# The 2048 x 2048 adjacency matrix enters on-chip memory through GpSimd's casting DMAs instead of float32 staging places

## What is computed

```python
x = layernorm(x + L0(x, adj))      # adj @ (x @ W) + b, eight heads side by side
x = layernorm(x + L1(x, adj))      # graph attention, 4 heads: softmax(leaky_relu(src+dst) + adj) @ (x @ W), mean
x = layernorm(x + L2(x, adj))      # two graph convolutions: relu([x, adj @ x] @ W + b), with a residual
x = layernorm(x + L3(x, adj))      # relu(D^-1/2 (adj + I) D^-1/2 @ x @ W)
```

## Time and profile before

| | |
|---|---|
| median of 3 runs | 685.37 us (685.23 to 685.78) |
| the profiled execution | 686.34 us, of which the profiled span is 684.6 us |
| TensorE matmul busy | 672.8 us, 98% of the span |
| VectorE, ScalarE, GpSimd busy | 76%, 57%, 24% |
| granted TensorE clock | 0.999 of full speed |
| SyncE's DMA queue | 39.37 MB |
| GpSimd's DMA queue | 7.34 MB |
| casts of the adjacency | 14 on ScalarE, 2 on VectorE |

### The profile page before, as it was taken

How to read it: one execution, slowest core, us unless ns; L and a number is a source line. 1 busy time by engine, 2 the same in 40 slices (tenths; PEclk the granted TensorE clock), 3 DMA queues, 4 the chain that set the end, 5 groups by cost and what they waited for, 6 DMA issues and landing times.

```text
span 684.6 us, 14405 instructions
## 1 busy us (share of the span) xinstructions
PE 672.8 (98%) x5326; PEld 511.9 (75%) x5326; DVE 522.6 (76%) x965; ACT 389.2 (57%) x499; POOL 163.9 (24%) x260
## 2 busy tenths in 40 slices
PE   8989999999999999999999999999999999999996
PEld 6878744788888888888888888884444468886444
DVE  5247668998998989989899898999454425874685
ACT  6556448798979889898898989643101000222000
POOL 4269627501001000010100001564021102442222
PEclk9999999999999999999999999999999999999999
DMA  8999431003003030030300303013021110211011
GB/s 334 380 404 302 83 105 33 16 1 77 18 33 61 26 66 0 31 61 31 61 0 31 61 0 63 1 36 72 17 54 24 24 23 18 40 39 32 32 51 42
DMA packets 48154, 47.65 MB, mean 70 GB/s; under 512 B 36017, under 2 KB 42225, under 8 KB 45937
## 3 DMA queue, kind: packets, MB, share of 16 engines
q1 hardware_dynamic: 45664, 39.37, 18.8%
q0 software_dynamic: 2016, 7.34, 5.7%
q10 hardware_dynamic: 432, 0.39, 0.2%
HBM read 29.23 MB, written 2.13 MB: 46 GB/s over the span
## 4 chain that ended last, share of the span: by engine, by line
PE 89%; DMA 4%; DVE 3%; ACT 2%; POOL 0%; issue 0%; ACTq 0%; SPq 0%; POOLq 0%
PE ps L725 16%; PE ps L727 16%; PE ps L726 16%; PE ps L571 16%; PE ps L561 9%; PE ps L573 6%; PE ps L574 6%; DMA arena<-in_adj 4%; PE ps L674 3%; DVE arena L1004 1%; ACT adj L413 1%; DVE ring_a L1048 1%; DMA arena<-in_x_turned 1%; DVE ring_hl L1053 0%; ACT ring_a L468 0%; ACT arena L447 0%
## 5 line engine op out<-in xcount | busy, mean ns | idle before, releaser
L727 PE MATMUL ps<-arena,ring_hl 128*128 (+1 forms) x1024 | 279.6, 273 | 0.0
L725 PE MATMUL ps<-arena,ring_hl 128*128 (+1 forms) x1024 | 278.8, 272 | 0.1
L726 PE MATMUL ps<-arena,ring_hl 128*128 (+1 forms) x1024 | 278.6, 272 | 0.0
L1048 DVE SCALAR_TENSOR_TENSOR ring_a<-rho,gam,ring_a 128x1024 f32<-128x1024 f32 x128 | 165.8, 1296 | 18.1 <-ACT ring_a L468 18.1
L1053 DVE TENSOR_TENSOR ring_hl<-ring_a,ring_hl 128x1024 f16<-128x1024 f32 x128 | 157.9, 1235 | 4.6 <-ACT ring_hl L482 4.6
L482 ACT ACTIVATE ring_hl<-ring_a 128x1024 f16<-128x1024 f32 x128 | 135.4, 1058 | 44.3 <-PE ps L727 27.4
L468 ACT ACTIVATE ring_a<-adj,shift 128x1024 f32<-128x1024 bf16 x128 | 146.0, 1141 | 0.0
L573 PE MATMUL ps<-arena,adj 128*128 128x257 f16 (+1 forms) x512 | 113.1, 273 | 3.0 <-ACT adj L413 3.0
L574 PE MATMUL ps<-arena,adj 128*128 128x256 f16 x512 | 113.1, 273 | 0.0
L571 PE MATMUL ps<-arena,adj 128*128 128x512 f16 x496 | 111.6, 379 | 0.0
L725 PEld LDWEIGHTS ps<-arena,ring_hl 128*128 128x128 f16 x1024 | 100.0, 98 | 13.0 <-DVE arena L1004 0.6
(11 more groups left out here) (109 smaller groups left out, 586.2 us busy)
## 6 DMA issues: line engine op xcount, KB each, us to landing
arena<-in_adj SPq DMA_DIRECT2D x16, 1024.0 KB, 10.7
x<-y POOLq DMA_DIRECT2D x14, 512.0 KB, 5.2
rho<-s_scratch SPq DMA_DIRECT2D x8, 512.0 KB, 3.7
x<-in_x SPq DMA_DIRECT2D x4, 512.0 KB, 17.0
out_x<-x SPq DMA_DIRECT2D x16, 128.0 KB, 1.7
arena<-in_x_turned SPq DMA_DIRECT2D x2, 512.0 KB, 6.2
arena<-in_L_gnn_W SPq DMA_DIRECT2D x1, 1024.0 KB, 11.3
arena<-in_L_gnn_a SPq DMA_DIRECT2D x1, 1024.0 KB, 13.3
```

Source lines behind the costliest of these rows:

```text
L725: nc.tensor.matmul(acc, hi, v_hi, start=(jt == 0), stop=False)
L726: nc.tensor.matmul(ps[:, b, 0:D], hi, v_lo, start=False, stop=False)
L727: ins = nc.tensor.matmul(acc, lo, v_hi, start=False, stop=(jt == T - 1))
L1048: nc.vector.scalar_tensor_tensor(a, rho[:, q, :], gam[:, at(h, 1), jt], a, op0=ALU.max, op1=ALU.mult)\
```

## The change

The staging places, the casts and their semaphores go. GpSimd issues 16 DMAs, one for each piece, that read float32 from the device's main memory and write bfloat16 straight into `adj`. `adj` now has the layout [partition, row tile, contraction tile, column], so that a piece is two runs of 1024 elements in each partition; the host orders the piece accordingly. Each piece has its own semaphore, and TensorE waits for that. SyncE holds back its loads of the bias and x until certain pieces have landed. GpSimd issues pieces 0 and 2 before its five low parts of `xt`, pieces 1, 3, 4, 5 between and behind them, then 6 and 7, 8 to 11 each behind an `add_b0`, and 12 to 15 ahead of its loop over tiles. ScalarE makes the high half of `w1` behind `gat_hi(4)`, ahead of that loop before. The row tiles of `rest` in the first layer are written out, with no loop.

```diff
-        adj = sb("adj", [P, T, N], BF16)
+        adj = sb("adj", [P, T, T, P], BF16)
...
-        STAGES = 4
-        SW = JH * LW
-        stage = part(arena, (PSET, PSET + STAGES * SW), F32, "p (s w) -> p s w", s=STAGES)
-        w1f = part(arena, (PSET + STAGES * SW, PSET + STAGES * SW + K2 * H * D), F32, "p (k h f) -> p k h f", k=K2, h=H)
-        o = PSET + STAGES * SW + K2 * H * D
+        o = PSET + T * D + K2 * H * D
+        w1f = part(arena, (PSET + T * D, o), F32, "p (k h f) -> p k h f", k=K2, h=H)
         w1ff = w1f.rearrange("p k h f -> p k (h f)")
-        xts = part(arena, (PSET + STAGES * SW, PSET + STAGES * SW + T * D), F32, "p (t c) -> p t c", t=T)
+        xts = part(arena, (PSET, PSET + T * D), F32, "p (t c) -> p t c", t=T)
...
-            for n in FIRST_LOADS:
-                load_adj(n)
+            sp.wait_ge(ld_adj[FIRST_LOADS[1]], 16)
             sp.dma_start(bias0, b0_in.rearrange("(a n) -> a n", a=1).partition_broadcast(P)).then_inc(ld_b, 16)
 
             def load_x(r):
                 sp.dma_start(x[:, r * R:(r + 1) * R, :], xr[:, r * R:(r + 1) * R, :]).then_inc(ld_x[r], 16)
             load_x(0)
-            load_adj(4)
-            load_adj(5)
+            sp.wait_ge(ld_adj[3], 16)
             load_x(1)
-            sp.wait_ge(s_lo, T)
+            sp.wait_ge(ld_adj[6], 16)
             sp.dma_start(w1f, w1_in.rearrange("(k p) (h f) -> p k h f", p=P, h=H)).then_inc(ld_w1, 16)
             sp.dma_start(abc.rearrange("p h s f -> p (h s f)"),
                          a_in.rearrange("h f a -> a (h f)").partition_broadcast(P)).then_inc(ld_a, 16)
-            load_adj(6)
-            load_adj(7)
             load_x(2)
-            load_adj(8)
+            sp.wait_ge(ld_adj[10], 16)
             load_x(3)
-            for n in range(9, NL - 2):
-                load_adj(n)
-            for n in range(NL - 2, NL):
-                load_adj(n)
...
-            for n in (1, 3, 4, 5):
-                cast_n(n)
-            w1_hi(0)
-            w1_hi(1)
-            cast_n(6)
-            CAST = cast_n
-            behind = {0: [(CAST, 7)], 2: [(CAST, 8)], 3: [(CAST, 9)], 4: [(CAST, 10)], 5: [(CAST, 11)], 6: [(CAST, 12)],
-                      7: [(CAST, 13)], 9: [(CAST, 14)], 10: [(CAST, 15)], 12: [(was_hi,)]}
+            behind = {4: [(w1_hi, 0), (w1_hi, 1)], 12: [(was_hi,)]}
...
-                nc.scalar.activation(ring_a[:, jt % SLOTS, :], adj[:, jt, q * CH:(q + 1) * CH], ACT.Exp,
+                nc.scalar.activation(ring_a[:, jt % SLOTS, :].rearrange("p (b c) -> p b c", b=BANKS), adj[:, q * BANKS:(q + 1) * BANKS, jt, :], ACT.Exp,
...
-                lhs = adj[:, j, at(it * P, P)]
+                lhs = adj[:, at(it, 1), j, :].rearrange("p a c -> p (a c)")
...
-                if knext in PLACES:
+                if knext in PLACES or a == 0:
...
-            def columns_cast(j):
+            def columns_loaded(j):
                 if j == 0:
                     pe.wait_ge(s_one, 1)
                 if j % JH == 0:
-                    pe.wait_ge(*cast_done(STAGES // 2 + j // JH))
-            joint(0, 0, lambda t: 0, columns_cast)
-
-            def cast_ready(t, u, half):
-
-                pe.wait_ge(s_cast_act, t + (half + 1 - u % 2 - STAGES // 2))
-            rest(0, None, cast_ready)
+                    for n in (j // JH, 2 + j // JH):
+                        pe.wait_ge(ld_adj[n], 16)
+            joint(0, 0, lambda t: 0, columns_loaded)
+
+            def piece_loaded(t, u, half):
+
+                pe.wait_ge(ld_adj[t // 2 * 2 + half], 16)
+            rest(0, None, piece_loaded)
...
-            casts_after = {8: 0, 11: 2}
             for t in range(T):
                 take(0, t, t % R)
-                if t in casts_after:
-                    cast_n(casts_after[t])
...
+            adj_n = adj_in.rearrange("c h p w -> (c h) p w")
+
+            def load_adj(n):
+                js = slice((n % 2) * JH, (n % 2 + 1) * JH)
+                nc.gpsimd.dma_start(adj[:, n // 2 * 2:n // 2 * 2 + 2, js, :],
+                                    adj_n[n].rearrange("p (i j c) -> p i j c", i=2, j=JH)).then_inc(ld_adj[n], 16)
+            pool.wait_ge(*xt_loaded(4))
+            load_adj(FIRST_LOADS[0])
+            load_adj(FIRST_LOADS[1])
             pool.wait_ge(s_lo, CHUNKS[5][0])
-            for lo, hi in CHUNKS[5:]:
+            later_loads = {0: FIRST_LOADS[2], 1: FIRST_LOADS[3], 3: 4, 4: 5}
+            for n, (lo, hi) in enumerate(CHUNKS[5:]):
                 pool.wait_ge(s_hi, hi)
                 nc.gpsimd.tensor_sub(xt[:, lo:hi, D:2 * D], xts[:, lo:hi, :], xt[:, lo:hi, 0:D]).then_inc(s_lo, hi - lo)
+                if n in later_loads:
+                    load_adj(later_loads[n])
+            load_adj(6)
+            load_adj(7)
             pool.wait_ge(ld_b, 16)
 
             def add_b0(t):
@@ -1169,6 +1135,8 @@
                 nc.gpsimd.tensor_tensor(x[:, t, :], x[:, t, :], bias0, ALU.add).then_inc(s_xb, 1)
             for t in range(2 * R):
                 add_b0(t)
+                if t >= R:
+                    load_adj(t + 4)
...
+            for n in range(12, NL):
+                load_adj(n)
```

More of the change, by code:

```diff
@@ L153, in graph_stack @@
         ld_xt = [sem(f"ld_xt{i}") for i in range(6)]
-        ld_adj = [sem(f"ld_adj{i}") for i in range(STAGES)]
+        ld_adj = [sem(f"ld_adj{i}") for i in range(NL)]
         ld_w0 = [sem(f"ld_w0{i}") for i in range(K2)]
@@ L219, in xt_loaded @@
             return ld_xt[next(n for n, (lo, hi) in enumerate(XT_LOADS) if lo <= t < hi)], 16
-        def cast_done(n):
-            if n < STAGES:
-                return (s_cast_act if n % 2 else s_cast), n // 2 + 1
-            return s_cast_act, n + 1 - STAGES // 2
-        def cast_of(n):
-            src = stage[:, n % STAGES, :].rearrange("p (j w) -> p j w", j=JH)
-            return adj[:, (n % 2) * JH:(n % 2 + 1) * JH, (n // 2) * LW:(n // 2 + 1) * LW], src
         PLACES = {3: {5: [0], 6: [1, 2], 7: [3, 4], 8: [5, 6], **{t: [t - 2] for t in range(9, T)}},
@@ L259, in _ @@
                     sp.dma_start(w0f[:, 1, :], w0r[:, 1, :]).then_inc(ld_w0[1], 16)
-            adj_n = adj_in.rearrange("c h p w -> (c h) p w")
-            def load_adj(n):
-                if n >= STAGES:
-                    sp.wait_ge(*cast_done(n - STAGES))
-                sp.dma_start(stage[:, n % STAGES, :], adj_n[n]).then_inc(ld_adj[n % STAGES], 16)
-            for n in FIRST_LOADS:
-                load_adj(n)
+            sp.wait_ge(ld_adj[FIRST_LOADS[1]], 16)
             sp.dma_start(bias0, b0_in.rearrange("(a n) -> a n", a=1).partition_broadcast(P)).then_inc(ld_b, 16)
@@ L611, in last_tile @@
                     for j in range(T):
-                        lhs = adj[:, j, (T - 1) * P:T * P]
+                        lhs = adj[:, T - 1, j, :]
                         for half, first in ((0, j == 0), (1, False)):
@@ L1271 @@
         host["adj"].T.reshape(halves, n // (halves * p), p, blocks, n // blocks).transpose(3, 0, 2, 1, 4)
-        .reshape(blocks, halves, p, -1))
+        .reshape(blocks, halves, p, n // (halves * p), -1, p).transpose(0, 1, 2, 4, 3, 5).reshape(blocks, halves, p, -1))
     host["L0_gnn_W"] = np.ascontiguousarray(host["L0_gnn_W"].transpose(1, 0, 2))
```

7 lines of the change are left out of this document (removed).

## The result

The changed kernel is slower: 698.69 us median of 4 runs (696.01 to 698.92) against 685.58 us for the kernel before on the same chip (685.23 to 686.57), ratio 1.018 [1.0157, 1.0203]. The prediction named 684.2 us, with a range of 682 to 702 us: the time is inside the range, but the sign is the other one, and the loss is 13.1 us where the likeliest case had a gain of 1.2 us.

What follows compares the result with a forecast made beforehand. TensorE was taken to bound the kernel; layer 1 would start at the later of its own 76.4 us and `was` at 77.5 us, against 78.7 us: -1.2 us, so 684.2 us from 685.37 us, range 682.0 to 702 us.

Steps and rivals of the forecast that it cites:

- the likeliest case: The forecast itself: issues of 0.95 to 1.2 us, casts at plain speed, 684.2 us (683.2 to 685.8), chance 0.36.
- 1.2 us were feared: Issues ahead of and among GpSimd's low parts: joint stage starts at 19.8 us, not 18.64 us, +0.6 to +3.9 us.
- about 27 us: Landing of x rows 4 to 7, asked for at about 22 us, before GpSimd's next adds ahead of its loop.
- part (b): Issues on GpSimd ahead of its loop over tiles: loop start moves from 34.92 us to 38.2 us.
- L: Start of GpSimd's loop over tiles, put at 38.2 us; `was` ready 39.3 us later, at 77.5 us.
- dear issues: Rival: GpSimd issues from 1.2 us up delay its loop; at 1.62 us, +5.3 us, 690.7 us; chance 0.20.
- The issue price: GpSimd's time for each of sixteen added issues: between 0.86 and 1.62 us, taken as 1.05 us.
- light issues: Rival: GpSimd issues cost 0.86 us each, loop starts at 36.7 us, -2.7 us, 682.7 us; chance 0.22.
- Casting transfers slow: Rival: from 3.5 us a piece TensorE waits; 4.5 us gives 699.7 us, 5.3 us gives 712.5 us; chance 0.22.
- VectorE's normalisation would lengthen an issue: By a two-port rule, the four issues of pieces 12 to 15 grow by up to 0.4 us each; sum about +0.4 us.
- The sum: TensorE starts layer 1 at 77.5 us against 78.7 us, moving the end one for one: -1.2 us, 684.2 us.
- the 3.0 us of waits for casts: TensorE's three waits for ScalarE's casts in the joint aggregation, expected to go: -3.0 us.

Runs made afterwards that it cites:

- Eight issues: Kernel before, with eight small DMAs into an unread tile issued by GpSimd where the changed kernel issues pieces 8 to 15: 687.86 us.
- the two with moved products: Products 0 and 1 ahead of the loop (all inputs early, x in 4 KB runs): 693.71 us; products two tiles forward (the version at piece 3): 691.37 us.
- the two with all inputs early: Changed kernel, SyncE asking for bias, x rows 0 to 7, `w1f`, `abc` straight behind the turned features: 693.88 us; with 4 KB runs of x too: 694.22 us.
- eps on ScalarE: The version at piece 3, with the addition of eps to the variance moved from GpSimd to ScalarE: 688.33 us.
- its layout: Kernel before with only the new layout of `adj`, staging places and casts kept: 685.63 us.
- late x: Kernel before, with SyncE asking for x rows 4 to 7 behind piece 7 instead of piece 5: 693.02 us.
- one queue: Changed kernel with bias, x, `w1f` and `abc` also issued by GpSimd, in the order of the kernel before, 23 issues instead of 16: 690.18 us.
- the issues first: Changed kernel, with GpSimd issuing pieces 8 to 15 behind piece 7, ahead of its wait for x: 696.11 us.
- x in 4 KB runs: Changed kernel, with x stored by the host so that four rows lie together, one 4 KB run per partition for each load: 695.82 us.
- `w1f` early: Changed kernel, with only `w1f` and `abc` asked for ahead of the wait for piece 2: 700.42 us.
- the version at piece 3: Changed kernel, with x rows 0 to 7 asked for at once and `w1f` and `abc` when piece 3 has landed instead of piece 6: 688.98 us.

## Why the prediction was wrong

**Right, by the rows.** TensorE's projections end where they did (18.6 us): moving pieces 0 to 5 among the low parts cost nothing, where 1.2 us were feared. The cast runs at the plain rate, 272 packets a piece at 638 in 6 us, 2.56 us for 2.6, and TensorE's L532 never waits for a piece. The layout is free. From the start of the loop to `was` it takes 85.36 - 46.10 = 39.3 us, the prediction's number to 0.1 us. And the end does hang on `was`, 0.1 us ahead of layer 1.

**Wrong: "about 27 us".** The step that failed is the term for the landing of x rows 4 to 7 in part (b), "which then share the DMA queues: about 27 us". It was 37.5 us, 10.5 us off. The request came as predicted; the transfers of x were sized as if each had its turn behind the bytes ahead of it, as in one queue at 0.41 MB/us, rows 0 to 3 (taken as landed by 22 us, used at 31.66 us) as well as rows 4 to 7. They stand in a second one, and there their packets of 1 KB go one for one with packets of 4 KB. With 37.54 us in place of 27 and an issue of 0.74 us, the prediction's own formula gives L = 37.54 + 4 x (0.70 + 0.74) + 4 x 0.74 = 46.3 us (46.10 measured) and `was` at 85.6 us. The mechanism had been named, at the end of the rival of dear issues ("a later landing of x rows 4 to 7 ... works at the same place, 1 us for 1 us"), but its size was never worked out, and it was given no chance of its own.

**The issue price erred the safe way.** 1.05 us were taken, 0.74 us came. So the price of the rival "light issues" (0.86 us) was the nearest and that of "dear issues" the wrong one; the loss came from the place that both shared. Eight issues by themselves cost 2.1 us in the kernel before. "Casting transfers slow" is excluded by 0.418 MB/us, and with it goes the reason for which the range reached beyond 691 us. Whether VectorE's normalisation would lengthen an issue no run shows: it stood behind the eight issues and not beside them.

**Missing: two steps behind `was`.** The sum took the end to move with the start of layer 1, one for one. It moved 6.9 us, and attention 12.96 us. First, the turned tiles: in the kernel before TensorE starts 2 us behind `was`, and never waits for one (an unbroken chain); where it starts right behind `was`, it meets tiles that come from the same loop a little later, 3.0 us in the changed kernel, 2.5 to 3.2 us in seven of its variants. The distance orders all the runs but the two with moved products: 0.1 us behind `was`, 2.5 to 3.2 us of waits; 1.0 to 1.1 us (the two with all inputs early), 1.6 us; 1.8 us (eps on ScalarE), 0.6 us; 1.9 to 2.0 us (the kernel before, its layout, late x and eight issues), 0 to 0.3 us. So no variant won the 3.0 us of waits for casts either: with `was` at 77.3 us and layer 1 at 77.40 us, attention began at 123.70 us, not before 122.20 us. Second, the clock: behind the waits of 2.55 and 0.46 us the 1.2 GHz level held from 96 to 102 us, +2.8 us. In the variant with waits of 1.97 and 0.50 us, the stretch behind them had the full clock:

```profile
88.00:92.00 4.00, 3.95 (x22) 1.88 (x23) 0.00 (x0) 0.60 (x1) 0.00 (x0) 1.00 0.17 33
```

and the remainder is gone: from the start of layer 1 to attention 46.30 us, against 43.65 us before plus 2.5 us of waits; in the changed kernel 49.70 us against 43.65 + 3.0. What decides whether the clock falls is open, and the length of the waits is not it: with 2.9 us of them (one queue) it stayed at 1.00, and of two variants with 2.5 us each, the issues first and x in 4 KB runs, one fell and the other did not (96 to 98 us in both):

```profile
96.00:98.00 2.00, 2.00 (x6) 0.76 (x5) 0.00 (x0) 0.60 (x1) 0.00 (x0) 0.50 0.01 1
...
96.00:98.00 2.00, 1.83 (x15) 0.92 (x16) 0.00 (x0) 0.01 (x1) 0.00 (x0) 1.00 0.34 66
```

Executions of one kernel differ too: of the changed kernel's four, three took 698.64 to 698.92 us at a mean clock of 0.989 to 0.992 and one 696.01 us at 0.994. These 2.7 us are the size of the clock's piece, though the short one has no trace.

**A regularity that holds it together.** In the kernel before the first product starts at 42.60 us and `was` is ready at 76.60 us:

```profile
42.60 1.27 POOL L1180 TENSOR_TENSOR ring_a<-arena 128x512 f32<-128x512 f32 x1
```

That is 34.0 us. After the change: 85.36 - 51.35 = 34.0 us. In ten runs in which only inputs or issues moved it lies between 34.0 and 34.1 us, from a first product at 45.51 us (the eight issues) to 54.85 us (`w1f` early); the version at piece 3 took 35.5 us, with 1.45 us of waiting for later rows of x. So the chain through GpSimd has no slack in that stretch: everything that delays its first product arrives at `was` in full.

**Shown and not shown.** Shown by single edits in the kernel before: late x alone loses 7.0 us, the issues alone 2.1 us, the layout nothing. Shown in the changed kernel: asking earlier for x and for `w1f` and `abc` together regains 9.7 us, x alone 3.9 us, `w1f` and `abc` alone, at the very front, nothing. That x is slow for its share of packets is shown by the equal counts and by the 4 KB runs (8.8 for 14.0 us). Argued from the traces, and not shown by an edit, is that the waits for turned tiles come from the start right behind `was`, and that the clock's 2.8 us belong to the stop. Open is what keeps the best variants 2.5 to 3.5 us behind in the median: their traces show attention only 1.1 and 1.5 us later, in executions of 687.39 and 687.60 us that were among the shortest. Some of it may be the eight issues, the turned tiles, the pieces or the clock; no run took the eight issues out of a version in which all inputs were in time.

## What to carry to other kernels

When a large stream moves to another engine's queue, work out anew when everything that stays in the old queue lands: what was ordered by position is now ordered by the waits that replace it, and where two queues are full, the one with the smaller packets falls behind (here a quarter of the engines' time for 1 KB against 4 KB). Look for the engine without slack (here GpSimd from its first product on), list its inputs in the order in which it needs them, and give each a landing time; if the first is mended the next one shows, as `abc` did behind x. And a stop of the bound engine can cost more than its length, for the clock behind it (here 2.8 us on top of 3.0 us). Last, a time inside the range proves no mechanism: here the range held it for a cause that did not occur.
